# A stage that joins a layer's two branches: tiles in pairs, one change of function tables for both, all products on VectorE

## What is computed

```python
vth = jnp.maximum(v_th, 0.1)
spike_p = jax.nn.sigmoid(10.0 * (y - vth))
s = (y * spike_p * jax.nn.silu(z)) @ W_out - xn
x_q = (xn / s_in).astype(float8_e4m3fn)            # made in an earlier stage, stored as bf16
k_q = (kernel / s_k).astype(float8_e4m3fn)
g = jax.nn.silu((x_q @ k_q) * (s_in * s_k) + bias)
x1 = x + s * g
```

## Time and profile before

| | before |
|---|---|
| median of 3 executions | 4021.08 us (4018.24 to 4024.04) |
| the profiled execution: its time | 3990.48 us |
| the profiled execution: its span, first to last instruction | 3988.9 us |
| the stage, from its first DMA issue to the end of its last VectorE instruction | 954.17 to 1135.47 us |
| first tile's tanh on ScalarE | 967.71 us |
| first `s` and last `s` on VectorE (16 of them) | 979.33 and 1130.27 us |

### The profile page before, as it was taken

The page is one execution under the profiler, slowest core; times in us unless marked ns, Lnnn a source line. Parts: engine busy times, 40 slices in busy tenths (PEclk is TensorE's granted clock), DMA queues, the critical chain, the costliest instruction groups (busy, mean ns, idle before and its releaser), DMA issues. The chain is left out here.

```text
span 3988.9 us, 64991 instructions
## 1 busy us (share of the span) xinstructions
PE 3377.5 (85%) x19711; PEld 2058.5 (52%) x19712; DVE 3155.0 (79%) x4214; ACT 2370.5 (59%) x4325; POOL 1366.7 (34%) x953
## 2 busy tenths in 40 slices
PE   8969898996669799797999999999999976299950
PEld 6745455553458688795333333333333324189940
DVE  7869999997866566477899999999999935277868
ACT  6668888886955433210577777777777761033323
POOL 7859998994014454301000000000000005744520
PEclk9989999998889899997799999999999996599975
DMA  7854444544869632394122323223223115222258
GB/s 262 283 187 164 159 163 166 179 146 166 280 174 255 164 111 74 109 291 134 27 54 62 69 53 72 58 55 75 54 60 71 30 21 178 87 86 89 90 175 293
DMA packets 531451, 521.11 MB, mean 131 GB/s; under 512 B 84784, under 2 KB 441264, under 8 KB 531040
## 3 DMA queue, kind: packets, MB, share of 16 engines
q1 hardware_dynamic: 517248, 480.45, 41.0%
q0 software_dynamic: 13952, 37.74, 2.7%
HBM read 301.15 MB, written 215.71 MB: 130 GB/s over the span
## 5 line engine op out<-in xcount | busy, mean ns | idle before, releaser
L2395 DVE TENSOR_REDUCE at_top<-at_psM 128x1 f32<-128x1024 f32 x1024 | 1205.1, 1218 | 101.5 <-PE at_psM L2254 99.8
L2363 ACT ACTIVATE at_probs<-at_psS 128x512 f32<-128x512 f32 x2048 | 1061.0, 603 | 286.0 <-PE at_psS L2280 286.0
L2280 PE MATMUL at_psS<-at_q,at_k 64*128 64x512 f32 x2048 | 803.4, 471 | 8.2 <-ACT at_probs L2363 8.1
L2254 PE MATMUL at_psM<-at_k,at_q 62*128 62x512 f32 x2048 | 704.9, 454 | 41.3 <-DMA at_vraw<-scratch_vf 22.0
L655 POOL TENSOR_TENSOR sc_prod<-sc_state,sc_c_row 128x1024 f32<-128x1024 f32 x256 | 648.8, 2564 | 84.1 <-DVE sc_state L806 72.2
L2254 PEld LDWEIGHTS at_psM<-at_k,at_q 62*128 62x128 f32 x2048 | 313.1, 190 | 621.4 <-DVE at_top L2395 539.3
L806 DVE TENSOR_TENSOR_SCAN sc_state<-sc_dec,sc_psI 128x1024 f32<-128x1024 f32 x256 | 574.2, 2276 | 43.6 <-PE sc_psI L727 34.0
L2293 PE MATMUL at_psV<-at_probs,at_v 128*32 128x512 f32 x4096 | 546.3, 605 | 0.0
L738 PE MATMUL sc_psY<-sc_prod,sc_ident 128*128 128x512 f32 x1024 | 480.5, 599 | 15.2 <-DVE sc_y L792 15.2
L2221 POOL COPY at_v<-at_vraw 128x256 f32<-128x256 f32 x32 | 12.8, 401 | 1249.4 <-DMA at_vraw<-scratch_vf 1166.6
L2280 PEld LDWEIGHTS at_psS<-at_q,at_k 64*128 64x128 f32 x2048 | 337.7, 184 | 170.3 <-ACT at_probs L2363 160.4
(11 more groups left out here) (409 smaller groups left out, 4904.4 us busy)
## 6 DMA issues: line engine op xcount, KB each, us to landing
sc_c_row<-scratch_bc SPq DMA_DIRECT2D x128, 512.0 KB, 3.7
scratch_xs<-at_zeros SPq DMA_DIRECT2D x140, 264.0 KB, 4.7
sc_b_row<-scratch_bc SPq DMA_DIRECT2D x32, 512.0 KB, 5.0
ec_y<-scratch_ys SPq DMA_DIRECT2D x32, 512.0 KB, 6.1
ex_x<-scratch_xs SPq DMA_DIRECT2D x39, 264.0 KB, 3.3
si_x<-in_x SPq DMA_DIRECT2D x16, 512.0 KB, 5.6
scratch_xn<-si_xn SPq DMA_DIRECT2D x16, 512.0 KB, 6.2
scratch_x_t<-si_xT SPq DMA_DIRECT2D x16, 512.0 KB, 3.1
```

What stands on the lines that cost most here:

```text
L2254: ins = pe.matmul(psM[t % 2][:, half * TILE:(half + 1) * TILE], rows_of(q4[j], h, 0, MAXROW)[:, c * P:(c + 1) * P], rows_of(k4[j], h, 0, M ...
L2280: pe.matmul(psS[v % 3][:], rows_of(k4[j], h, 0, GROUP)[:, c * P:(c + 1) * P], rows_of(q4[j], h, 0, GROUP)[:, half * TILE:(half + 1) * TILE ...
L2363: act.activation(probs[:, slot(j, v), :], psS[v % 3][:], ACT.Exp).then_inc(act_done, 1)
L2395: dve.tensor_reduce(top[j % 2][:, h, c:c + 1], psM[t % 2][:], AX.X, ALU.max, negate=True).then_inc(maxed, 1)
```

## The change

Two neighbouring tiles, p = 2j and q = 2j+1, form pair j (8 pairs), and all four engines' programs are written out by pair, with no loop. VectorE keeps the same nine operations per tile, each in a function of its own (`spiked`, `opened`, `gated`, `biased`, `denominator`, `silu`, `residual`, `weighted`, `joined`). ScalarE loads one set of tables that holds both Exp and Ln for the Exp, Ln and Exp of both tiles. `ysp`, `zsp`, `g0`, `gs`, `gden`, `g`, `glog` and `sg` get a second buffer, `g1` gets four. `x` and `xn` get separate semaphores. On SyncE the first two tiles are loaded ahead of the weights, and the loads of `x` and `xn` are taken apart: `xn` comes last in a turn. The core of the diff (the waits that only protect a buffer from being overwritten are `later(...)`, a wait that is left out where its value is not positive):

```diff
+            # SyncE
+                load_yz(0)
+                load_yz(1)
                 sp.dma_start(wout[:], halves(A["w_out"])).then_inc(weights, 16)
...
                 sp.dma_start(xmax[:], A["xmax"]).then_inc(weights, 16)
-                def step(i, k):
-                    if not known(i) or i:
-                        store(i - 1, (k + 1) % 2)
-                        if not known(i) or i + 1 < NT:
-                            load_x(i + 1, (k + 1) % 2)        # x and xn
-                    if not known(i) or i + SETS < NT:
-                        sp.wait_ge(a_ready, i + 1)
-                        sp.wait_ge(g_psum, i + 1)
-                        m.settle(sp)
-                        load_yz(i + SETS, k)
...
-                turns(sp, step)
-                store(NT - 1, (NT - 1) % 2)
+                load_yz(2)
+                load_yz(3)
+                for i in two:
+                    load_xn(i)
+                    load_x(i)
+                for i in two:
+                    sp.wait_ge(a_ready, i + 1)
+                    sp.wait_ge(g_psum, i + 1)
+                    m.settle(sp)
+                    load_yz(i + SETS)
+                for j in range(PAIRS):
+                    for i in pair(j - 1):
+                        store(i)                              # waits for x1(i)
+                        if i + 2 < NT:
+                            load_x(i + 2)
+                    for i in pair(j + 1):
+                        if i + SETS < NT:
+                            sp.wait_ge(a_ready, i + 1)
+                            sp.wait_ge(g_psum, i + 1)
+                            m.settle(sp)
+                            load_yz(i + SETS)
+                    for i in pair(j):
+                        if i + 2 < NT:
+                            sp.wait_ge(s_ready, i + 1)
+                            m.settle(sp)
+                            load_xn(i + 2)
+                for i in pair(PAIRS - 1):
+                    store(i)
+            # ScalarE
+                for i in pair(0):
+                    spikes(i)
+                act.wait_ge(tok_ready, 1)
+                for i in pair(0):
+                    product(i)
+                for j in range(PAIRS):
+                    p, q = pair(j)
+                    for i in pair(j + 1):
+                        spikes(i)
+                    act.preload_act_table_set("natural_log_exp_and_others")
+                    exponential(p)
+                    exponential(q)
+                    if j + 1 < PAIRS:
+                        product(p + 2)
+                    logarithm(p)
+                    logarithm(q)
+                    if j + 1 < PAIRS:
+                        product(q + 2)
+                    reciprocal(p)
+                    reciprocal(q)
+            # TensorE
+                for i in pair(0):
+                    gate(i)
+                for j in range(PAIRS):
+                    for i in pair(j):
+                        out(i)
+                    for i in pair(j + 1):
+                        gate(i)
+            # VectorE
+                def residual(i):
+                    dve.wait_ge(o_psum, i + 1)
+                    dve.wait_ge(xn_loaded[i % 2], 16 * (i // 2 + 1))
+                    later(dve, sg_ready, i - 1)
+                    dve.tensor_tensor(s[i % 2][:], psO[i % 2][:], xn[i % 2][:], ALU.subtract).then_inc(s_ready, 1)
...
+                for i in pair(0):
+                    spiked(i)
+                    opened(i)
+                    gated(i)
+                for i in pair(0):
+                    biased(i)
+                for j in range(PAIRS):
+                    p, q = pair(j)
+                    more = j + 1 < PAIRS
+                    for i in pair(j - 1):
+                        silu(i)
+                        weighted(i)
+                    if more:
+                        spiked(p + 2)
+                    residual(p)
+                    if more:
+                        opened(p + 2)
+                        gated(p + 2)
+                        spiked(q + 2)
+                    denominator(p)
+                    if more:
+                        opened(q + 2)
+                    denominator(q)
+                    residual(q)
+                    if more:
+                        gated(q + 2)
+                        biased(p + 2)
+                    for i in pair(j - 1):
+                        joined(i)
+                    if more:
+                        biased(q + 2)
+                for i in pair(PAIRS - 1):
+                    silu(i)
+                    weighted(i)
+                    joined(i)
```

More of the change, by code:

```diff
@@ L853, in rows, with later, pair @@
             return A[name].rearrange("(i s p) d -> i p s d", p=P, s=SUB)[i, :, :, :]
[L855 to L869, removed]
+        def later(eng, sem, value):
+            if value > 0:
+                eng.wait_ge(sem, value)
+        def pair(j):
+            return [i for i in (2 * j, 2 * j + 1) if 0 <= i < NT]
         with nc.Block() as block:
@@ L880, in _ @@
                 sp.dma_start(xmax[:], A["xmax"]).then_inc(weights, 16)
[L882 to L889, removed]
@@ L920, in _, with spikes @@
                 act.wait_ge(vbias_ready, 1)
[L922 to L926, removed]
+                def spikes(i):
+                    k = i % SETS
+                    act.wait_ge(yz_loaded[k], 48 * (i // SETS + 1))
+                    later(act, ysp_ready, i - 1)
                     for h in range(H):
@@ L940, in step, with exponential @@
-                def step(i, k):
+                        t = i * SUB + c
+                        act.activation(g0[i % 2][:, c, :], psG[i % 2][:, c, :], ACT.Copy,
+                                       scale=per_tok[:, t:t + 1]).then_inc(g0_ready, 1)
+                def exponential(i):
                     act.wait_ge(g1_ready, i + 1)
-                    if not known(i) or i:
-                        act.wait_ge(gden_ready, i)
-                    act.activation(gs[:], g1[k % 2][:], ACT.Exp, scale=-1.0).then_inc(gs_ready, 1)
+                    later(act, gden_ready, i - 1)
+                    act.activation(gs[i % 2][:], g1[i % SETS][:], ACT.Exp, scale=-1.0).then_inc(gs_ready, 1)
@@ L950, in step @@
[L950 to L957, removed]
-                act.wait_ge(tok_ready, 1)
-                product(0, 0)
-                turns(act, step)
+                    later(act, g_ready, i - 1)
@@ new lines, in biased, with denominator @@
+                def biased(i):
+                    dve.wait_ge(g0_ready, SUB * i + SUB)
+                    later(dve, g_ready, i - SETS + 1)
+                    later(dve, gs_ready, i - SETS + 1)
+                    dve.tensor_tensor(g1[i % SETS][:], g0[i % 2][:], over_chunks(bias[:]), ALU.add).then_inc(g1_ready, 1)
+                def denominator(i):
+                    dve.wait_ge(gs_ready, i + 1)
+                    later(dve, glog_ready, i - 1)
+                    dve.tensor_scalar(gden[i % 2][:], gs[i % 2][:], 1.0, None, ALU.add).then_inc(gden_ready, 1)
@@ L1038, in joined, with weighted @@
+                def weighted(i):
                     dve.wait_ge(g_ready, i + 1)
                     dve.wait_ge(s_ready, i + 1)
[L1040 to L1046, removed]
-                        dve.wait_ge(x1_st[par], 16 * (i // 2))
@@ L1073, in _ @@
-                front(0, 0)
-                turns(dve, step)
-                opened(NT - 1, (NT - 1) % 2)
-                joined(NT - 1, (NT - 1) % 2)
+                    later(dve, x1_ready, i - 1)
+                    dve.tensor_tensor(sg[i % 2][:], s[i % 2][:], g[i % 2][:], ALU.mult).then_inc(sg_ready, 1)
+                for i in pair(0):
[4 more added lines that the diff above has]
+                    biased(i)
```

130 lines of the change are left out of this document (55 added, 75 removed).

## The result

The changed kernel takes 4058.08 us (median of 4, 4054.25 to 4065.62) against 4020.51 before (median of 4). The ratio is 1.0095 with a 95% interval of 1.0076 to 1.0114: 38 us slower. The forecast was 4049, slower, with 4035 to 4063 as its range.

What follows compares the result with a forecast made beforehand. Bound before: a ring of VectorE and ScalarE; after: late `xn` in SyncE's queue. 999.5 + 4 x 27.6 + 2 x 20.8 + 12.3 = 1163.8 against 1135.5, so 4021.1 + 28.3 = 4049, range 4035 to 4063.

Steps and rivals of the forecast that it cites:

- The lag from `x1` to `s`: SyncE's turn: 1.0 to first packet, 7.2 stores and `x`, 6.8 `y`, `z`, `xq`, 1.4 `xn`, 0.6 release: 17.0 us.
- six times 4.7: Balance in the `xn`-in-time rival: it decides where the lag sinks below 12.3, six times 4.7 being the 28.3 us.
- the rival of a served-out-of-order queue: At `residual(p)`: DMA engines serve `xn` beside earlier issues, landing within 6.6 us of E; no stall, 4001; chance 0.08.
- that of a DMA bound: Rival stated for moving `xn` ahead: 17 us of traffic per pair bounds, the wait moves to other loads, 4030 or more.
- The start: Stage start: weights behind six tile loads land 3.4 us later, first tanh moves from 967.7 to 971.1, `residual(2)` at 999.5.
- The shadow that I gave the weights' issue: Stage start: weights' delay taken as 3.4 us, between 0 (all issued in the shadow of others) and 5.
- the walk: Stage start, operation by operation from first tanh at 971.1 to `residual(2)` at 999.5, its `xn` landed by about 998.
- R + 12.3: Stage end: `joined(15)` is done 12.3 us after R, the start of the last pair's `residual`; `joined(14)` waits for tile 12's store.
- Tables worth nothing with the stall: ScalarE: 33 table loads become 15 or so, 23 us saved, but worth nothing while VectorE stalls 10.4 us per pair.
- left to itself: VectorE's new order without the stall: 17.2 us per pair against 20.5, winning 3.3 us per pair.
- the first rival: `xn` arrives in time at `residual(p)`: no stall, pairs of 17.2 us, stage end 1115.0, 20.5 less, 4001; chance 0.08.

Runs made afterwards that it cites:

- The run with `xn` between: Changed kernel with the `xn` loads issued behind stores and `x` but ahead of `y`, `z`, `xq`; 4028.45 us, ratio 1.0019.
- the repaired kernel: Changed kernel with weights first and, in each SyncE turn, `xn`, then `y`, `z`, `xq`, then the stores with `x`; 3999.59 us, ratio 0.9947.

## Why the prediction was right, point by point

*Direction and mechanism.* The named wait, `residual(p)` for `xn`, is the one that came. The lag from `x1` to `s` was put at 17.0 us and is 17.0 in the pair shown. That it agrees to a tenth is luck: two stores and two `x` took 6.6 us where 7.2 stood, and from the last packet of `xn` to the start of `s` it took 1.0 where 0.6 stood. The other terms held to 0.2. The periods of the four turns with `y` and `z` were put at 27.6 and are 27.62, 27.82, 28.05 and 27.65; the two without at 20.8, and are 20.95 and 20.93. `s` of odd tiles never waits. ScalarE's predicted 15 loads are 15. One sum among the rivals was wrong: two of the six stalls were put at 3.6, so six times 4.7 cannot be saved, and the lag at which gain and loss balance is about 10, not 12.3. The run with `xn` between, at 10.15, bears that out. The forecast did not rest on it. The three runs that move `xn`, between, ahead, and onto another queue, leave neither the rival of a served-out-of-order queue nor that of a DMA bound: order in one queue decides, and free bandwidth does not help a load that has not been asked for.

*Size.* The forecast was 28.3 us longer in the stage, the trace shows 36.5. The stage began 0.9 later in this execution, which is no part of the change. The other 7.3 come from these terms.

- The start, 4.5 of them. I put the weights 3.4 us later and `s` of tile 2 at 45.3 after the stage's first issue (999.5 less 954.17). The weights were 6.8 later, outside the 0 to 5 that I allowed, and `s` started 49.8 after it. The shadow that I gave the weights' issue did not exist: their small transfers queued behind 2.6 MB, and the last landed 8.0 us after its issue at 961.61, where before it took 4.9. The 6.8 that I had for the 2.6 MB was the delay.
- In the same place, a step of the walk was wrong and not only its size: "its `xn`, with no store ahead, has landed by about 998". It was issued at 997.36, behind `y` and `z` of tile 7, which wait for `a` of tile 3, and VectorE idled 3.45 us for it. The queue rule that carried the rest of the prediction held here too, and I had not walked the first turn by it. These two misses make 6.8 and only 4.5 show, because my walk was 2.3 too long elsewhere: 1.1 of it is a wait of ScalarE for TensorE that did not come, the rest mostly the overlap of neighbouring operations on ScalarE. That part of the agreement is luck too.
- The end, 1.7. R + 12.3 was 14.0: `joined(14)` waited 2.54 us for `x`, which SyncE asks for only after the store of tile 12. I had looked at the store's landing and not at the load behind it. The periods add 1.0.

*Tables worth nothing with the stall.* Shown, by 20.5 us of loads put back at 2.7. In the repaired kernel two further loads lengthened a pair from 17.12 to 18.48 us; ScalarE's 16.3 busy us of a pair and 2 x 1.283 would be 18.9 at most. The Trainium skill, "ScalarE: Activation LUTs", section "What ACT_TABLE_LOAD costs", gives 2.66 with the drain; by it the two further loads alone would bring the pair to an estimated 21.5 (16.2 + 2 x 2.66). The trace disagrees, as it did before the change.

*17.2 us per pair without the stall.* The forecast's "left to itself" and the first rival's spacing were right (17.13). That rival gave 4001 for a kernel without the wait, and the kernel with weights and `xn` put right takes 3999.6. The nearness of these two is in part chance, since the rival still had the weights late: the run that moves `xn` alone takes 4003.5.

## What to carry to other kernels

When a loop is regrouped, write the DMA queue's new order beside the order of use: a wait in a queue delays everything behind it, and a load whose buffer has long been free is late if it stands behind a store that waits for the end of the computation. Take the lag as the bytes issued ahead and its own, divided by the measured rate, and a start and a release (1.0 us each here), and do so for the first and last turn too. A saving on one engine shows only in what is left once the longest wait is gone, so mend the order of the queue before judging the rest of a change.

## What was not expected

A sum moved to an idle engine made the busy engine slower. `gden`, 0.42 us alone, took up to 2.57 us beside GpSimd's sum, and the kernel lost some 8 to 10 us where 0 to 13 of gain were thought possible. And the three bounds of the repaired stage lie close together: over five whole pairs VectorE is busy 0.99 of the time, ScalarE 0.95 and the DMA engines 0.93.
